# Attention: in each step the exponential's tile goes ahead of the leading tile, with the relation chain's first part and sums moved to match

## What is computed

```python
q = (x @ Wq.T + bq).reshape(b, s, h, hd)        # k, v alike
attn_scores = jnp.einsum('bihd,bjhd->bhij', q, k) / scale
li = x @ rel_W[:, :d].T
lj = x @ rel_W[:, d:].T
logits = li[:, :, None, :] + lj[:, None, :, :] + rel_b
relation_probs = jax.nn.softmax(logits, axis=-1)
bias = jnp.einsum('bijk,hk->bhij', relation_probs, logical_bias)
gate = jax.nn.sigmoid(x @ gate_W.T + gate_b)
attn_scores = attn_scores + gate * bias
attn_weights = jax.nn.softmax(attn_scores, axis=-1)
out = jnp.einsum('bhij,bjhd->bihd', attn_weights, v).reshape(b, s, d)
```

## Time and profile before

| | us |
|---|---|
| three runs: lowest, median, highest | 3251.27, 3261.2, 3266.76 |
| the profiled execution's own time | 3259.23 |
| its span, first to last instruction | 3257.4 |

### The profile page before, as it was taken

One profiled execution on the slowest core, in us unless ns is written; L12 is line 12 of the kernel. 1 busy time (PEld: TensorE's weight loads), 2 busy tenths in 40 slices (PEclk: granted clock), 3 DMA queues, 4 the chain that ended last, 5 costly groups with the idle time before them and its releaser, 6 DMA issues.

```text
span 3257.4 us, 122555 instructions
## 1 busy us (share of the span) xinstructions
PE 2989.6 (92%) x53463; PEld 2278.3 (70%) x53463; DVE 2433.3 (75%) x3495; ACT 2033.3 (62%) x2669; POOL 2283.7 (70%) x1528
## 2 busy tenths in 40 slices
PE   4389999999999999994999999999999999999998
PEld 2267777777777777772677777777777777777776
DVE  4777777777777777734878778787877878787775
ACT  2345555555555555552677777777777777777775
POOL 1635555555555454306999999999999999999995
PEclk8589999999999999997999999999999999999999
DMA  5544445444444444404322233223223322322221
GB/s 116 101 80 86 77 84 88 85 79 86 81 83 84 78 84 84 84 5 124 82 64 63 69 79 83 59 68 96 66 67 81 83 58 69 94 68 67 68 76 45
DMA packets 253990, 251.90 MB, mean 77 GB/s; under 512 B 81999, under 2 KB 198624, under 8 KB 253328
## 3 DMA queue, kind: packets, MB, share of 16 engines
q1 hardware_dynamic: 251776, 243.67, 35.4%
q10 hardware_dynamic: 1680, 0.40, 0.1%
HBM read 96.22 MB, written 40.37 MB: 42 GB/s over the span
## 4 chain that ended last, share of the span: by engine, by line
PE 38%; ACT 8%; issue 4%; DVE 1%; POOL 1%; SPq 0%; DMA 0%; ACTq 0%; DVEq 0%; POOLq 0%
PE R L1235 11%; PE R L1242 10%; PE R L1345 5%; PE R L1259 5%; PE R L1333 4%; ACT kT L1364 3%; ACT sq L1376 3%; ACT kT L1369 2%; PE psB L1314 2%; PE R L1255 1%; PE psA L1308 0%; DVE mx L1513 0%; DVE ssq L1538 0%; DVE k L1504 0%; DMA xs_f<-xm 0%
## 5 line engine op out<-in xcount | busy, mean ns | idle before, releaser
L660 ACT ACTIVATE prob<-psS 128x1024 f32<-128x1024 f32 x512 | 524.0, 1024 | 598.7 <-PE psS L537 591.2
L824 DVE TENSOR_TENSOR colmax<-psS,colmax 128x1024 f32<-128x1024 f32 x480 | 587.3, 1224 | 309.1 <-PE psS L537 307.9
L537 PE MATMUL psS<-diag,pst 128*128 128x64 bf16 x16384 | 585.9, 195 | 26.6 <-issue 26.4
L1235 PE MATMUL R<-wqkv,xsT 128*128 128x512 f32 x1152 | 573.2, 620 | 37.1 <-ACT sq L1376 31.3
L537 PEld LDWEIGHTS psS<-diag,pst 128*128 128x128 f16 x16384 | 519.1, 99 | 87.3 <-issue 33.9
L529 PE MATMUL psS<-qst,kst 48*128 48x128 bf16 (+1 forms) x8192 | 382.0, 221 | 125.6 <-DMA pst<-p_parts 89.9
L758 POOL TENSOR_TENSOR rel<-rel,rec 128x1024 f32<-128x1024 f32 x64 | 151.7, 2370 | 484.7 <-DVE rec L837 484.7
L1364 ACT ACTIVATE kT<-R 64x1024 f32<-64x1024 f32 x192 | 195.7, 1019 | 423.7 <-PE R L1242 422.6
L529 PEld LDWEIGHTS psS<-qst,kst 48*128 48x128 bf16 (+1 forms) x8192 | 236.1, 95 | 282.4 <-issue 173.0
L1235 PEld LDWEIGHTS R<-wqkv,xsT 128*128 128x128 f32 x1152 | 196.9, 190 | 227.4 <-issue 159.6
L571 PE MATMUL psO<-prob,v 128*9 128x128 f32 x8192 | 326.6, 275 | 12.6 <-issue 11.3
(11 more groups left out here) (190 smaller groups left out, 6076.2 us busy)
## 6 DMA issues: line engine op xcount, KB each, us to landing
v<-vs SPq DMA_DIRECT2D x576, 128.0 KB, 2.4
pst<-p_parts SPq DMA_DIRECT2D x512, 128.0 KB, 4.9
p_parts<-stage SPq DMA_DIRECT2D x64, 512.0 KB, 3.0
v<-vs SPq DMA_DIRECT2D x384, 64.0 KB, 2.0
wqkv<-in_L_ffn_Wqkv SPq DMA_DIRECT2D x18, 512.0 KB
q_stack<-qpart SPq DMA_DIRECT2D x6, 512.0 KB
qst<-q_stack SPq DMA_DIRECT2D x32, 96.0 KB, 5.4
wo<-in_L_ffn_Wo SPq DMA_DIRECT2D x6, 512.0 KB
```

Of the source, the lines that this page charges most:

```text
L537: last = pe.matmul(o, pst[:, par, g, P * jb:P * (jb + 1)], diag[:, par, g, h0:h0 + HH // 2, :], start=False, stop=(g == NG - 1), skip_grou ...
L660: act.activation(prob[:, st % 2, :], psS[:, slot_of("b", st)].rearrange("p a b -> p (a b)"), ACT.Exp)\
L824: dve.tensor_tensor(dst, src, dst, ALU.max).then_inc(a_read, 1)
L1235: last = pe.matmul(R[slot[kind, n]][:, c, :], xsT[:, n % 3, :], w[:, INNER * which + 512 * c:INNER * which + 512 * (c + 1)], start=True, s ...
```

## The change

On PE the B tile's score matmuls and its 16 relation matmuls go ahead of A's, with their waits; slots are given in the order B0 A0 B1 A1 .... `first_part` moves on ACT from behind window step 2 to behind window step 4. On POOL `total` goes ahead of `low_part`. No operation is added or taken away.

```diff
@@ -486,13 +486,13 @@
             if st < 0:
                 return st % 3
-            return (2 * st + (kind == "b")) % 3
+            return (2 * st + (kind == "a")) % 3
 
         def tiles(first, last):
 
             earlier = [("a", s) for s in range(-LEAD, 0)] if first else \
-                [(kind, s) for s in range(-4, 0) for kind in "ab"]
-            now = [(kind, s) for s in range(4 * NB) for kind in "ab" if kind == "b" or not (last and s + LEAD >= 4 * NB)]
+                [(kind, s) for s in range(-4, 0) for kind in "ba"]
+            now = [(kind, s) for s in range(4 * NB) for kind in "ba" if kind == "b" or not (last and s + LEAD >= 4 * NB)]
@@ -607,17 +607,17 @@
                     tile_a, tile_b = psS[:, slot_of("a", st)], psS[:, slot_of("b", st)]
-                    if ahead:
-                        wait_a(al, ja, it * 2 + al // 2)
-                        wait_slot(it, held["a", st])
-                        queries_keys(tile_a, apar, ahalf, ja, GUARD_ROW)
                     if jb == 0:
                         pe.wait_ge(guard_dma, (it * 4 + ul + 1) * 16 * 2)
                     wait_slot(it, held["b", st])
                     queries_keys(tile_b, par, half, jb, GUARD_ROW + 3)
                     if ahead:
+                        wait_a(al, ja, it * 2 + al // 2)
+                        wait_slot(it, held["a", st])
+                        queries_keys(tile_a, apar, ahalf, ja, GUARD_ROW)
+                    relations(tile_b, par, half, jb).then_inc(b_done, 1)
+                    if ahead:
                         relations(tile_a, apar, ahalf, ja).then_inc(a_done, 1)
-                    relations(tile_b, par, half, jb).then_inc(b_done, 1)
@@ -707,12 +707,12 @@
                     if opens and o == 0:
                         clamp(n, q, r, par)
-                    if closes and o == 2:
-                        first_part(n - 1, 1 - r)
                     if opens and o == 2:
                         third(n, r)
                     if opens and o == 3:
                         pair_exp(n, r, par)
+                    if closes and o == 4:
+                        first_part(n - 1, 1 - r)
@@ -778,10 +778,10 @@
                     if opens:
                         pair_args(n, q, r)
+                    if opens:
+                        total(n, r)
                     if closes:
                         low_part(n - 1, 1 - r)
-                    if opens:
-                        total(n, r)
```

## The result

Four executions of the changed kernel took 3339.64 to 3358.09 us, median 3355.53, against a median of 3256.23 for the kernel before beside them: a ratio of 1.0309, interval 1.0285 to 1.0332. It is 3.1% slower, outside my range and on the side that I gave 0.24. The profiled execution took 3355.38 us (before: 3259.23), with a span of 3353.5 us and a mean granted clock of 0.953.

A forecast was written before the change was run, and what follows sets the result against it. PE is busiest in the attention phase, its plain steps held by DVE's maximum. Terms -38 + 31 - 12 + 11 + 4 + 1 + 3 = 0 gave 3259 us; own range 3236 to 3283, with rivals 3220 to 3292.

The forecast's parts named there:

- Plain steps: Attention phase: B before A shortens a plain step from 2.29 to 2.15 us, 38 us gained over 271 steps.
- The guard's step: Steps 11 to 14 of a unit: later DVE chain and transposition, R of 14 1.03 us later, 31 us lost.
- Step 14, the guard's issues: Step 14: DMA issues on ACT's queue delay exponential 13, so PE waits 1.40 us between the two score groups.
- The first rival: The guard's DMAs do not reach PE, exponential 13 runs at its own time: 3224 us, chance 0.15.
- outT: Step 1: value matmuls wait for DVE's later copy of psO and start 0.37 us late, 11 us lost.
- The diagonal: POOL's diagonal, behind low_part in each fourth window, ends later and delays step 8: 14 x 0.27 = 4 us lost.
- The gaps: PE's "issue" gaps move with the pst bursts to where PE waits anyway: 12 us given back (none to 28).
- Late loads: Rival: pst loads come late, PE waits 2 us before A of step 20 in 15 blocks: 3289 us, chance 0.13.
- first_part's move: ACT: keeps first_part (about 0.95 us) out of window step 2; about 1 us in all reaches PE.
- the 0.07: Plain step: the 0.07 us ACT has to spare, as R could come at 2.08 and PE needs 2.15.

The follow-up runs named there:

- e3_total_waits: The changed kernel, but in the windows of a unit's second half POOL's total waits until DVE's guard chain is done: 3264.34 us, ratio 1.0045.
- e6_wait_and_sp: The changed kernel with total waiting for the guard chain and the guard's two DMAs issued by SP instead of ACT: 3264.47 us, ratio 1.0028.
- the best version: Kernel before plus PE's new order and slots, total waiting for the guard chain, SP issuing the guard's DMAs, outT copied at step 0's end: 3232.12 us.

## Why the prediction was wrong

- *Plain steps:* right. 2.15 from R to R, with the times of ACT and DVE within it. The medians of steps 2, 6, 7, 8, 10 and 15 went from 2.29 to 2.15 or 2.16. Step 5 is an exception, 2.41 instead of 2.29.
- *The guard's step:* this is the step that failed. I moved DVE's chain by 0.46 us and kept its length, "its last one starting 2.88 after the maximum did", from a trace in which POOL was idle beside it. In the same prediction I had total start at once behind the pair of exponentials and end at 5.6, and the chain run until 4.20; I never laid the two beside each other. With total kept away, the step is as I worked it out: a median of 2.92 in e3_total_waits (2.36 in some units) against 5.03 - 2.15 = 2.88. With total beside the chain, the median is 7.24.
- *What the trace of before could tell:* `largest` (L829) lasts 0.74 in most windows, but more than twice that where it starts beside `scaled`, as here in the timeline of the kernel before:

```profile
594.34 2.37 POOL L758 TENSOR_TENSOR rel<-rel,rec 128x1024 f32<-128x1024 f32 x1 [8.97 <-DVE rec L837]
...
595.61 1.65 DVE L829 SCALAR_TENSOR_TENSOR top<-f,own,top 128x512 f32<-128x512 f32 x1
```

  My sum took no notice of it. The Trainium skill has it ("SBUF — State Buffer", Who interferes with whom): VectorE shares a pair of ports with GpSimd. By the Trainium skill, an instruction with two SBUF inputs contends with a GpSimd instruction that reads SBUF, and copies, casts and scalar operations can where they run in a mode that takes both ports, of which it says "Whoever issues first gets the shared pair for the whole instruction". The runs agree: 0.17 us become 1.1 to 2.0, up to the end of POOL's operation, and the maxima, whose other input is in PSUM, and the reciprocals keep their 1.22 and 0.94 beside POOL. It is the rule against this change that I should have weighed.
- *Step 14, the guard's issues:* right in kind and size. 3.44 in e3_total_waits against 8.58 - 5.03 = 3.55. In the changed kernel it is less, since the collision holds PE and ACT alike. The first rival, that the issues don't reach PE, is refuted: taking them off ACT's queue took 34.3 us out of step 14 (98.8 to 64.5).
- *outT:* 11 us forecast, 13.0 measured. *The diagonal:* in the changed kernel step 8 of a block's first unit lasts 2.54 to 2.66 in 10 of 15 blocks and 2.18 to 2.20 in the others: 4.6 us in all, where I had 4. In e6_wait_and_sp it is 2.18 in all 15, before any edit to the diagonal.
- *The gaps:* the 12 us that I took as given back did not come. They moved, out of steps 9 and 10 (28.1 us less) and into 11 and 12 (19.2 more) among others, but PE's idle time charged to "issue" ahead of its score, relation and value matmuls stayed: 49.9 us before, 51.6 in the changed kernel, 49.7 in e3_total_waits.
- *Late loads:* they did not happen in the changed kernel, where no wait of PE for pst stands in the phase. low_part ended 7.7 us after R of a window's step 3, as I had it. They cost 7.1 us with total waiting and 28.0 once step 14's stall was gone too.
- *first_part's move:* I called it needed because the 0.07 would be passed. In window step 2 a transposition always gives ACT more room, and the best version has first_part there with 1.3 us of waits. My working didn't look at that step.
- *The range:* it left out a change in the length of an operation whose neighbours move, and step 13 is 91 of the 96 us. The rest of the sum came out 11 us too low: with the collision gone (e3_total_waits) the phase is 11.4 us longer than before, where I had 0, and the missing 12 of the gaps is about that much, though no run shows that the two are the same. The bounds that I listed also add up to 3234 to 3276, not to 3236 to 3283.

## What to carry to other kernels

When work on DVE or POOL moves by even half a microsecond, lay the two engines' new timelines side by side, and count a short DVE operation that can be held (the last section has which were) as lasting until the POOL operation beside it ends. A chain of small dependent operations is worst: it can pay again for each POOL operation beside it. Compare the engines' busy times and the mean length of each group with those of before, since no view of waits shows such a hold. When a chain that others wait for is hit so, an added wait on the other engine is cheap; here it was worth more than the change itself. And a transfer that hides behind a stall is a cost as soon as the stall is gone.

## What the hardware showed

- A cast from fp32 to bf16 or a subtraction of 8 columns takes 0.17 us alone and 1.1 to 2.0 when it starts just behind a POOL operation of 1.3 to 2.1 us, ending 0.02 to 0.04 us after it; a single operation slips in between two of POOL's. Not held beside POOL were the cast from bf16 to fp32 of 24 columns (L875, 0.18 in all 28 cases of the kernel before), the reciprocals, the reductions and the maxima out of PSUM.
- After PE had stood for 4.3 us, its granted clock was at the lower level, half of full speed. In the 18 units where PE waited 2.96 us or more for the guard, the relation matmuls behind the wait took 1.84 to 1.89 us; in the 11 where it waited 1.53 us or less, 1.11. The stretches of the changed kernel around the wait of 4.3 us (PEclk is the number ahead of the DMA share):

```profile
689.00:695.00 6.00, 2.27 (x70) 1.78 (x64) 5.83 (x7) 3.25 (x5) 4.47 (x3) 0.88 0.01 3
696.00:699.00 3.00, 3.00 (x56) 2.66 (x58) 0.97 (x3) 0.63 (x1) 0.00 (x0) 0.50 0.56 182
```

  The relation matmuls of step 13 then last 1.89 us instead of 1.11, so such a stall costs 0.8 us there beyond its own length, and somewhat more with the scores and values. The change's mean clock, 0.953 against 0.972, is a consequence of the waits: with total waiting it was back at 0.971.
- A DMA of 3 KB issued 2.4 us after the first of eight loads of 128 KB took 5.9 us to reach its reader.
